# The last batch of a fused graph layer: first picked rows transposed and split inside the gates, last state turned back two products on, second-layer banks in a new order

## The chip, the cores and the metric

One Trainium2 chip, one of its cores. The metric is the device time of one execution in microseconds (us), as the median of several runs. All eight batches of the problem are worked on by this one core, one behind the other.

The engines are named as the profile names them: PE is the matrix engine (PEld its weight loads), DVE the vector engine, ACT the scalar engine, POOL the GpSimd engine, SP the queue that issues the transfers. An order such as `up` or `gelu` is a function of the kernel; its line numbers are those of the kernel before.

## The reference

Two layers with a residual each. The second one is what the change is about: it runs on rows picked by a learned weight.

```
x = x + gnn(layernorm(x), adj, ...)          # 8 x 1024 x 128
x = x + ffn(layernorm(x), ...)

# the end of gnn: a GRU cell
gi = x_in @ w_ih.T + b_ih ;  gh = x @ w_hh.T + b_hh
r = sigmoid(gi_r + gh_r) ;  z = sigmoid(gi_z + gh_z)
n = tanh(gi_n + r * gh_n)
return (1 - z) * n + z * x

# ffn: only the rows with the greatest weights, 511 of the 1024 of a batch
weights = x @ wr + br
idx  = top_k(weights, 512)[:, :511]
sel  = x[idx]
y    = (gelu(sel @ w1 + b1) @ w2 + b2) * weights[idx]
return x with y added at idx
```

## The kernel before

Each engine has its own program, written out by hand in order, and they meet at semaphores (`wait_ge`). An engine does nothing behind an instruction that waits. The graph layer is computed batch by batch (`step`, 8 times) with features on the 128 partitions and nodes along the free axis in two halves of 512. At the end of a batch come the **gates**: `gru` and `gru_rest` multiply, for half 0 and then half 1, the weights of the reset, update and new gate into the banks M0, M1, D0, D1 (half 0) and C0, C1, N0, N1 (half 1). Each product of float32 quality is three matmuls (`three`, L1361 to L1363), since both operands are kept as a coarse part and a rest (`xTH` and `xTL`). ACT applies the tanh of the gates (`gates`: `ga` L815, `tr` L818, `tz` L820), DVE adds up the new gate (`new_gate`, L1039 and L1042), ACT takes its tanh (`candidate`, L825), POOL forms state less candidate (`state_less_candidate`, L520), DVE blends (`blend`, L1048 and L1050), PE turns the new state back to nodes (`state_back`, L1455, eight transposes into two banks) and DVE adds it to x (`state_to_nodes`, L1081). Of the last batch there follow DVE's statistics (`moments2` L937, `mean_and_variance` up to `ve` L951), POOL's power (`inv_std2`, L534), and on DVE the norm (`last_norm`, L1300), the node weights (`node_weights`, L1116 to L1119), the base rows (L1315) and the ranks.

Behind the eight batches come nine **groups** of 512 picked rows (`over_groups`, `ffn_step`): groups 0 to 6 are the picked rows of batches 0 to 6, loaded from DRAM by SP (`load_sel`, L433) into the buffer of the adjacency, groups 7 and 8 are all rows of the last batch, whose unpicked rows are masked at the end. A group is: four transposes into bank D0 (`sel_to_features`, L1593), a coarse copy by ACT (`hi_of_sel`, L880) and the rest by DVE (`lo_of_sel`, L1258), four products up (`up`, three matmuls each, banks in rotation over `up_banks`), gelu on ACT (`gelu`, L887) and four products down (`down`, L1615, a float32 matmul that the trace shows as x2). `up(b, p, j)` waits for `lo_of_sel` of its group, and for the gelu that frees its bank; `down(b, p, j)` waits for the gelu of its tile. The picked rows of a group need the ranks of a batch, which DVE finds with counts over the row of weights (`rank`, L1129, L1135 and L1136; tile t takes three of them). In the last batch DVE has ranks of batch 6 between the steps of the gates: 1 to 3 before `new_gate(7, 0)`, 4 and 5 around `blend(7, 0)`, 6 and 7 in `ffn_step` 0, ahead of `blend(7, 1)`, `lo_of_sel` of group 1 and `state_to_nodes`.

In `ffn_step` 0 the PE does: `sel_to_features(0)`, three `up`, then for j = 0 the fourth `up`, `down`, `sel_to_features(1)` and `state_back(7)`; for j = 1 `down` and the first `up` of group 1; for j = 2 and 3 an `up` of group 1 and a `down` each.

Of the kernel before, what the change touches and what calls it, by code (L numbers as in the profile page):

```python
# [143 lines left out]
def build(nc, x, adj, vectors, weights, conv2_w, const, out):  # L144
    ctx = ExitStack()
    with ctx:
# [161 lines left out]

        up_banks = (C0, C1, D1)
        LU = len(up_banks)  # L310

        def wait(eng, s, b, per, k):
# [351 lines left out]
        def _(act):  # L664
# [144 lines left out]
            def gates(b, h):  # L809
# [10 lines left out]
                nc.scalar.activation(tz[:, h, :], z[:, :], ACT.Tanh, bias=col(V_GB + 1), scale=0.5).then_inc(tz_ok, 1)  # L820

            def candidate(b, h):
                wait(act, q2_ok, b, NH, h + 1)
                wait(act, back_ps, b - 1, NH, NH)
                nc.scalar.activation(gn[:, h, :], ga[:, h, :], ACT.Tanh, bias=col(V_BIH + 2)).then_inc(gn_ok, 1)  # L825
# [13 lines left out]
            def step(b, q, first, last):  # L839
# [31 lines left out]
                gates(b, 0)  # L871
                candidate(b, 0)
                gates(b, 1)

            over_batches(act, step)


            def hi_of_sel(b, p):
                wait(act, t_ps, b, 1, 1)
                nc.scalar.activation(xTH[:, 0, half(p)], D0[:, :], ACT.Copy).then_inc(xsH_ok, 1)  # L880

# [13 lines left out]
            def ffn_step(b, q, first, last):  # L895
                if first:
                    hi_of_sel(0, 0)
                gelu(b, q, 0)
                if first:
                    candidate(B - 1, 1)  # L900
                    hi_of_sel(1, 1)
                gelu(b, q, 1)
                gelu(b, q, 2)
                if not first and not last:
                    hi_of_sel(b + 1, 1 - q)
                if b == 2:
                    row_of_weights(B - 1, 0, M1)
                if not first:
                    update(b - 1, 1 - q)
                gelu(b, q, 3)  # L910
                if b == 2:
                    row_of_weights(B - 1, 1, M1)
# [6 lines left out]
        def _(dve):  # L919
# [108 lines left out]
            def common_added(b, k):  # L1028

                wait(dve, cc_ps, b, 2, k + 1)  # L1030
                wait(dve, g1_ok, b, 1, 1)
                cc = (N0[:, Q:2 * Q], N1[:, 0:Q])[k]
                STT(phases(GS[k]), on_phases(cc), col(V_SC2), phases(G1), ALU.mult, ALU.add).then_inc(gs_ok, 1)  # L1033

            def new_gate(b, h):
# [130 lines left out]
            def step(b, q, first, last):  # L1166
# [79 lines left out]
                blend(b, 0)  # L1246
                if last:
                    rank(b - 1, 0, 5)
                elif not first:
                    rank(b - 1, 1 - q, 4)  # L1250
                    indices(b - 1, 1 - q, 0)

            over_batches(dve, step)


            def lo_of_sel(b, p):
                wait(dve, xsH_ok, b, 1, 1)
                TT(xTL[:, 0, half(p)], D0[:, :], f32(xTH[:, 0, half(p)]), ALU.subtract).then_inc(xsL_ok, 1)  # L1258

# [59 lines left out]
            def ffn_step(b, q, first, last):  # L1319
                if first:  # L1320
                    new_gate(B - 1, 1)
                    lo_of_sel(0, 0)
                    rank(B - 2, 0, 6)
# [32 lines left out]
        def _(pe):  # L1356
# [75 lines left out]
            def conv_odd(b):  # L1432
# [16 lines left out]
                i.then_inc(c2_ps, 1)  # L1449

            def state_back(b, bank_):
                for h in range(NH):
                    wait(pe, o_ok, b, NH, NH)
                    for k in range(TH):
                        i = TR(bank_[h][:, k * P:(k + 1) * P], gn[:, h, k * P:(k + 1) * P], ident)  # L1455
                    i.then_inc(back_ps, 1)
# [81 lines left out]
            def gru_rest(b, h, q, parts, last):  # L1538
# [6 lines left out]
                else:  # L1545
                    wait(pe, nmL_ok, b, NH, NH)
                three(nh[:, :], wh(2), *X, True, True).then_inc(gate_ps, 1)
                three(ni[:, :], wi(2, 0), *XC, True, False)
                wait(pe, nmL_ok, b, NH, h + 1)
# [32 lines left out]

            def sel_to_features(b):
                if b < NXS:
                    pe.wait_ge(sel_in[b], 16)
                else:
                    pe.wait_ge(xn2_ok, B)
                if b == 0:
                    pe.wait_ge(q2_ok, NH * (B - 1) + 1)
                wait(pe, xsL_ok, b - 1, 1, 1)  # L1590
                for c in range(TH):
                    rows = Xs[:, b, c, 0:D] if b < NXS else R[:, 1, (b - NXS) * TH + c, 0:D]
                    i = TR(D0[:, c * P:(c + 1) * P], rows, ident)  # L1593
                i.then_inc(t_ps, 1)

            def up(b, p, j):
                wait(pe, xsL_ok, b, 1, 1)
                k = HT * b + j
                if k < LU:
                    pe.wait_ge((tr_ok, tz_ok, ga_ok)[k], NH * B if k < 2 else NH * (B - 1) + 1)  # L1600
                else:
                    pe.wait_ge(g_ok, k - LU + 1)
# [25 lines left out]
            def ffn_step(b, q, first, last):  # L1628
                if first:
                    sel_to_features(0)  # L1630
                    for k in range(LU):
                        up(0, 0, k)
                for j in range(HT):
# [5 lines left out]
                    if first and j == 0:  # L1639
                        sel_to_features(1)  # L1640
                        pe.wait_ge(tz_ok, NH * (B - 1) + 1)
                        pe.wait_ge(ga_ok, NH * B)
                        state_back(B - 1, (M1, N1))
                    if first and j == 1:
                        up(1, 1, 0)
                    if j == 1 and not first:
# [32 lines left out]
```

## Time and profile before

| | |
|---|---|
| Median of 3 runs | 565.66 us (565.02 to 565.83) |
| The profiled execution's own time | 567.16 us |
| Its span in the trace | 564.2 us |
| PE busy | 546.7 us, 97% of the span |
| DVE busy | 481.7 us, 85% |
| ACT busy | 354.2 us, 63% |
| POOL busy | 275.9 us, 49% |
| Mean granted clock of PE | 0.993 of full speed |

The trace begins with the first instruction and ends with the last; some 3 us of the profiled execution's time lie outside it. A row of the timeline gives start and duration in us, engine, line, operation, written tile <- read tiles, shape and count; in square brackets stands how long the engine had been idle and what released it. Buffer numbers are left out there, so that D is D0 or D1. Instructions of one engine overlap a little: the next one starts some 0.1 us (DVE, ACT) or 0.16 us (PE) before the one ahead of it ends. A row of the windows gives a stretch, its length, the busy time of PE, PEld, DVE, ACT and POOL with their instructions, then the granted clock of PE (1.00 is 2.4 GHz, 0.50 is 1.2 GHz), the DMA share and GB/s.

### The profile page before, as it was taken

Reading aid. Unit: us, or ns where it says so; the run is one execution under the profiler, and the core shown is the slowest. Engines: PE = TensorE matmul, PEld = TensorE weight load, DVE = VectorE, ACT = ScalarE, POOL = GpSimd, SP = SyncE. Lnnn points to the kernel's source line nnn. Section 1 sums busy time; section 2 is a strip of 40 time slices with the busy share of each in tenths; the row PEclk is TensorE's granted clock in tenths of the full one; section 3 lists DMA queues with packets and bytes.
Section 4 is the critical chain, followed back from the end, with each engine's and each line's share of the span. In section 5 each row is a group of like instructions: output and inputs, shape, how many; then the busy total and the mean of one; then the engine's idle time right before and its main releaser. Section 6 shows DMA issues by size and latency. Waiting matters only on the chain.

```text
span 564.2 us, 9042 instructions
## 1 busy us (share of the span) xinstructions
PE 546.7 (97%) x2964; PEld 417.2 (74%) x2964; DVE 481.7 (85%) x1064; ACT 354.2 (63%) x616; POOL 275.9 (49%) x346
## 2 busy tenths in 40 slices
PE   6899999999999999999999999999999999899996
PEld 3786788678966896689767976798678866666563
DVE  6997479689998999899999999899979987978722
ACT  4856475856686577748674858485857573555552
POOL 2740353325368335834484547554535265546552
PEclk9899999999999999999999999999999999999999
DMA  8602700180008300640056002800180006402111
GB/s 290 261 1 76 299 0 2 46 309 20 2 0 281 130 2 1 220 192 1 1 142 268 1 2 59 316 2 1 46 314 15 1 4 192 142 16 80 34 37 60
DMA packets 33339, 54.52 MB, mean 97 GB/s; under 512 B 2098, under 2 KB 23051, under 8 KB 33166
## 3 DMA queue, kind: packets, MB, share of 16 engines
q1 hardware_dynamic: 29710, 48.42, 24.6%
q0 software_dynamic: 3584, 5.54, 2.8%
q8 instruction: 23, 0.38, 0.3%
q14 instruction: 22, 0.18, 0.1%
HBM read 44.21 MB, written 13.43 MB: 102 GB/s over the span
## 4 chain that ended last, share of the span: by engine, by line
PE 84%; DVE 10%; ACT 3%; issue 2%; DMA 0%; POOL 0%; DVEq 0%; ACTq 0%; POOLq 0%
PE N L1510 19%; PE M L1487 10%; PE C L1361 7%; PE C L1362 7%; PE C L1363 7%; PE N L1615 6%; PE D L1481 5%; PE N L1361 3%; PE N L1362 3%; PE N L1363 3%; ACT hab L671 2%; DVE tr L1011 2%; PE D L1361 2%; PE M L1362 2%; PE M L1361 2%
## 5 line engine op out<-in xcount | busy, mean ns | idle before, releaser
L777 ACT ACTIVATE tr<-D 128x512 f32<-128x512 f32 x128 | 76.2, 596 | 76.8 <-PE D L1481 70.0
L1487 PEld LDWEIGHTS M<-cst,adjb 128*128 128x128 f32 x512 | 63.7, 141 | 36.5 <-issue 19.8
L1481 PE MATMUL D<-V,U 128*128 128x512 f32 x128 | 89.3, 697 | 0.0
L1487 PE MATMUL M<-cst,adjb 128*128 128x128 f32 x512 | 76.9, 273 | 1.3 <-DVE ga L1105 0.9
L575 POOL DMA_INDIRECT sel<-R,ridx x56 | 61.2, 1092 | 16.0 <-issue 13.8
L1510 PE MATMUL N<-tz,msgF 128*128 128x512 f32 x128 | 64.2, 593 | 0.0
L1510 PE MATMUL N<-ga,msgF 128*128 128x512 f32 x128 | 64.2, 593 | 0.0
L1361 PE MATMUL C<-zR,wc 128*128 128x256 f32 x208 | 61.0, 293 | 0.0
L1362 PE MATMUL C<-zR,wc 128*128 128x256 f32 x208 | 58.9, 283 | 0.0
L1363 PE MATMUL C<-zR,wc 128*128 128x256 f32 x208 | 58.8, 283 | 0.0
L1135 DVE TENSOR_SCALAR_CACHE_REDUCE junk<-W,R 128x1024 bf16<-128x1024 f32 (+3 forms) x64 | 51.6, 807 | 3.9 <-ACT W L739 2.1
L1105 DVE TENSOR_TENSOR ga<-tr,M 128x512 f32<-128x512 f32 x64 | 43.5, 680 | 10.7 <-ACT tr L777 10.0
L1105 DVE TENSOR_TENSOR tz<-tr,M 128x512 f32<-128x512 f32 x64 | 43.6, 683 | 7.3 <-ACT tr L777 3.3
L621 POOL TENSOR_TENSOR wk<-tz,xT 128x512 f32<-128x512 f32 x8 | 12.5, 1566 | 70.8 <-DVE tz L1033 70.8
L520 POOL TENSOR_TENSOR ga<-xT,gn 128x512 f32<-128x512 f32 x16 | 22.8, 1424 | 44.9 <-ACT gn L825 44.1
L1129 DVE TENSOR_SCALAR_CACHE_REDUCE junk<-W,R 128x128 bf16<-128x128 f32 (+6 forms) x56 | 41.3, 738 | 0.0
L1481 PEld LDWEIGHTS D<-V,U 128*128 128x128 f32 x128 | 24.3, 190 | 22.9 <-ACT tr L777 17.4
L602 POOL TENSOR_TENSOR junk<-hab 128x521 f32<-128x521 f32 x16 | 20.1, 1258 | 41.5 <-ACT hab L671 41.5
L1362 PEld LDWEIGHTS C<-zR,wc 128*128 128x128 f32 x208 | 39.8, 191 | 0.0
L1361 PEld LDWEIGHTS C<-zR,wc 128*128 128x128 f32 x208 | 39.6, 190 | 0.2 <-issue 0.2
L1363 PEld LDWEIGHTS C<-zR,wc 128*128 128x128 f32 x208 | 39.7, 191 | 0.0
L586 POOL DMA_INDIRECT out<-xn,adjb x28 | 28.4, 1014 | 20.8 <-DVE xn L1290 14.4
(237 smaller groups left out, 1537.1 us busy)
## 6 DMA issues: line engine op xcount, KB each, us to landing
adjb<-in_adj SPq DMA_DIRECT2D x8, 4096.0 KB, 14.9
adjb<-sel SPq DMA_DIRECT2D x7, 516.0 KB, 5.8
xall<-in_x SPq DMA_DIRECT2D x7, 512.0 KB
out<-R SPq DMA_DIRECT2D x7, 512.0 KB
R<-in_conv_w SPq DMA_DIRECT2D x1, 1088.0 KB, 6.9
sel<-R,ridx POOLq DMA_INDIRECT x56
xall<-in_weights SPq DMA_DIRECT2D x1, 832.0 KB, 9.4
xall<-in_x SPq DMA_DIRECT2D x2, 256.0 KB, 2.7
```

Of the source, the lines that this page charges most:

```text
L575: nc.gpsimd.indirect_dma_start(sel[b], bass.IndirectOffsetOnAxis(ap=ridx[:, q, t:t + 1], axis=0), R[:, q, t, :], None, bounds_check=KEEP - ...
L777: nc.scalar.activation(E[:, u % NE, :], Db[u % NH][:, :], ACT.Exp, scale=-1.0).then_inc(exp_ok, 1)
L1105: TT(A[u % NA], E[:, u % NE, :], Mb[u % NH][:, :], ALU.mult).then_inc(A_ok, 1)
L1129: TS(junk[:, t % 2, 0:t * P], W[:, 0:t * P], R[:, q, t, R_W:R_W + 1], None, ALU.is_ge, ALU.add, accum_out=acc[:, 0, t:t + 1])
L1135: TS(junk[:, k, t * P:N], W[:, t * P:], w, None, ALU.is_gt, ALU.add, accum_out=acc[:, 1, t:t + 1])
L1361: MM(out_, wgt(0), hi, start=start, stop=False)
L1362: MM(out_, wgt(0), lo, start=False, stop=False)
L1363: return MM(out_, wgt(1), hi, start=False, stop=stop)
L1481: MM(Db[h][:, :], U[:, t * P:(t + 1) * P], V[:, half(h)], start=True, stop=True).then_inc(d_ps, 1)
L1487: i = TR(Mb[h][:, k * P:(k + 1) * P], adjb[:, h * TH + k, t * P:(t + 1) * P], ident)
L1510: MM(Nb[h][:, :], msgF[:, t, :], A[v % NA], start=t == 0, stop=t == T - 1).then_inc(nm_ps, 1)
L1615: i = MM(Nb[p][:, :], wf2[:, j, :], g[p][j], start=j == 0, stop=j == HT - 1)
```

## The change

It touches only the end of the last batch and the first group.

1. **First picked rows.** `sel_to_features(0)` moves on PE from behind the gates into those of the second half, behind the state's product of the new gate (`nh`, bank N1), and writes bank M0 in place of D0 (`sel_bank`). `hi_of_sel(0, 0)` moves on ACT from behind the last gates to between `candidate(7, 0)` and `gates(7, 1)`. `lo_of_sel(0, 0)` moves on DVE from behind `new_gate(7, 1)` to behind `blend(7, 0)`, ahead of `rank` 5.
2. **Banks.** `up_banks` is (D1, C0, C1) in place of (C0, C1, D1), so that the first product up doesn't wait for the gates of the second half.
3. **State back.** `state_back(7)` moves on PE from behind `sel_to_features(1)` to behind `down(0, 2)`.

No instruction is added or taken away.

```
-        up_banks = (C0, C1, D1)
+        up_banks = (D1, C0, C1)
...
+        def sel_bank(b):
+            return M0 if b == 0 else D0
...
                 gates(b, 0)
                 candidate(b, 0)
+                if last:
+                    hi_of_sel(0, 0)
                 gates(b, 1)
...
                 blend(b, 0)
                 if last:
+                    lo_of_sel(0, 0)
                     rank(b - 1, 0, 5)
...
+            def sel_to_features(b):
+                if b < NXS:
+                    pe.wait_ge(sel_in[b], 16)
+                else:
+                    pe.wait_ge(xn2_ok, B)
+                if b == 0:
+                    pe.wait_ge(tr_ok, NH * (B - 1) + 1)
+                if b == 1:
+                    pe.wait_ge(q2_ok, NH * (B - 1) + 1)
...
                 three(nh[:, :], wh(2), *X, True, True).then_inc(gate_ps, 1)
+                if last and h == 1:
+                    sel_to_features(0)
                 three(ni[:, :], wi(2, 0), *XC, True, False)
...
-                    pe.wait_ge((tr_ok, tz_ok, ga_ok)[k], NH * B if k < 2 else NH * (B - 1) + 1)
+                    pe.wait_ge((ga_ok, tr_ok, tz_ok)[k], NH * B if k > 0 else NH * (B - 1) + 1)
...
                 if first:
-                    sel_to_features(0)
                     for k in range(LU):
                         up(0, 0, k)
...
                     if first and j == 0:
                         sel_to_features(1)
+                    if first and j == 1:
+                        up(1, 1, 0)
+                    if first and j == 2:
                         pe.wait_ge(tz_ok, NH * (B - 1) + 1)
                         pe.wait_ge(ga_ok, NH * B)
                         state_back(B - 1, (M1, N1))
-                    if first and j == 1:
-                        up(1, 1, 0)
```

PE in the gates of the second half, before and after (L1363 and L1367 end the new gate's product of the state, N0 takes its part of the convolved features, C0 the reset gate's part of the messages):

```order
L1363 MATMUL N1<-xTH,wall 128x512
L1361 MATMUL N0<-zR,wall 128x512
L1362 MATMUL N0<-zR,wall 128x512
L1363 MATMUL N0<-zR,wall 128x512
L1361 MATMUL C0<-V,wall 128x512
```

```order
L1367 MATMUL N1<-xTH,wall 128x512
L1467 MATMUL M0<-cst,adjb 128x128 x4
L1365 MATMUL N0<-zR,wall 128x512
L1366 MATMUL N0<-zR,wall 128x512
L1367 MATMUL N0<-zR,wall 128x512
L1365 MATMUL C0<-V,wall 128x512
```

The four transposes of the first picked rows now stand ahead of twelve matmuls of the gates.

PE in the first group, from `down(0, 0)` on, before and after (L1615 and L1623 are products down, L1593 and L1467 the picked rows of group 1, L1455 and L1474 the state):

```order
L1615 MATMUL N0<-xall,msgF 128x512
L1593 MATMUL D0<-cst,adjb 128x128 x4
L1455 MATMUL M1<-cst,gn 128x128 x4
L1455 MATMUL N1<-cst,gn 128x128 x4
L1615 MATMUL N0<-xall,msgF 128x512
L1361 MATMUL C1<-xTH,wall 128x512
L1362 MATMUL C1<-xTL,wall 128x512
L1363 MATMUL C1<-xTH,wall 128x512
L1361 MATMUL D1<-xTH,wall 128x512
```

```order
L1623 MATMUL N0<-xall,msgF 128x512
L1467 MATMUL D0<-cst,adjb 128x128 x4
L1623 MATMUL N0<-xall,msgF 128x512
L1365 MATMUL C0<-xTH,wall 128x512
L1366 MATMUL C0<-xTL,wall 128x512
L1367 MATMUL C0<-xTH,wall 128x512
L1365 MATMUL C1<-xTH,wall 128x512
L1366 MATMUL C1<-xTL,wall 128x512
L1367 MATMUL C1<-xTH,wall 128x512
L1623 MATMUL N0<-xall,msgF 128x512
L1474 MATMUL M1<-cst,gn 128x128 x4
L1474 MATMUL N1<-cst,gn 128x128 x4
```

Behind the picked rows of group 1 there is now nothing between the transposes and `down(0, 1)`; the state stands two products up and one product down later.

ACT from the candidate of the first half on, before and after (L815 and L819 are `ga`, L880 and L828 the coarse copy of picked rows):

```order
L825 ACTIVATE gn<-ga,vec 128x512
L815 ACTIVATE ga<-N1,vec 128x512
L818 ACTIVATE tr<-C0,vec 128x512
L820 ACTIVATE tz<-C1,vec 128x512
L880 ACTIVATE xTH<-D0 128x512
L887 ACT_TABLE_LOAD
L887 ACTIVATE xall<-C0,vec 128x512
```

```order
L833 ACTIVATE gn<-ga,vec 128x512
L828 ACTIVATE xTH<-M0 128x512
L819 ACTIVATE ga<-N1,vec 128x512
L822 ACTIVATE tr<-C0,vec 128x512
L824 ACTIVATE tz<-C1,vec 128x512
L893 ACT_TABLE_LOAD
L893 ACTIVATE xall<-D1,vec 128x512
```

The copy of the first picked rows now stands ahead of the three gates of the second half, and the load of the gelu table right behind them.

## Rows read from the trace of the kernel before

**Rows 1.** The page, the chain that ended last by engine.
```profile
PE 84%; DVE 10%; ACT 3%; issue 2%; DMA 0%; POOL 0%; DVEq 0%; ACTq 0%; POOLq 0%
```

**Rows 2.** Timeline of PE, last gates and first group: start, us, engine, instruction.
```profile
484.21 0.39 PE L1361 MATMUL N<-zR,wall 128*128 128x512 f32 x1
...
489.74 0.50 PE L1361 MATMUL C<-xTH,wall 128*128 128x512 f32 x1 [2.15 <-DVE xTL L1258]
...
495.08 0.60 PE L1593 MATMUL D<-cst,adjb 128*128 128x128 f32 x4
...
496.95 1.12 PE L1615 MATMUL N<-xall,msgF 128*128 128x512 f32 x2 [0.39 <-ACT xall L887]
...
498.14 0.40 PE L1362 MATMUL C<-xTL,wall 128*128 128x512 f32 x1
```

**Rows 3.** Windows: length, busy of PE, PEld, DVE, ACT, POOL, then granted clock.
```profile
8.00:11.31 3.31, 1.28 (x8) 0.87 (x9) 3.08 (x11) 1.97 (x4) 1.63 (x5) 1.00 1.03 337
17.00:19.00 2.00, 0.00 (x0) 0.00 (x0) 2.00 (x2) 0.57 (x1) 2.00 (x2) 1.00 1.02 408
20.50:23.30 2.80, 2.80 (x14) 2.62 (x14) 2.80 (x3) 2.75 (x5) 2.72 (x3) 0.50 0.90 358
491.30:494.40 3.10, 3.10 (x8) 2.27 (x7) 3.03 (x9) 0.74 (x2) 1.28 (x1) 0.50 0.00 1
```

**Rows 4.** Timeline of ACT, end of the gates.
```profile
486.49 0.69 ACT L820 ACTIVATE tz<-C,vec 128x512 f32<-128x512 f32 x1
487.63 0.60 ACT L880 ACTIVATE xTH<-D 128x512 fp32r<-128x512 f32 x1 [0.45 <-issue]
488.24 1.28 ACT L887 ACT_TABLE_LOAD   x1
```

**Rows 5.** SP's loads of picked rows: forms, first and last start, time to landing.
```profile
L433 SPq DMA_DIRECT2D adjb<-sel x7: 359/427/523, 471.2 to 509.3; - x7
...
DMA to landing us min/median/max: 4.2/5.8/7.2
```

**Rows 6.** Timeline of DVE, from the blend of the first half on.
```profile
485.46 0.69 DVE L1050 SCALAR_TENSOR_TENSOR gn<-ga,gn 128x512 f32<-128x512 f32 x1
...
489.00 0.68 DVE L1258 TENSOR_TENSOR xTL<-D,xTH 128x512 fp32r<-128x512 f32 x1
...
492.53 1.02 DVE L1136 SCALAR_TENSOR_TENSOR junk<-W,R,cst 128x128 bf16<-128x128 f32 x1
...
494.60 0.69 DVE L1050 SCALAR_TENSOR_TENSOR gn<-ga,gn 128x512 f32<-128x512 f32 x1
496.35 0.69 DVE L1258 TENSOR_TENSOR xTL<-D,xTH 128x512 fp32r<-128x512 f32 x1 [1.06 <-ACT xTH L880]
496.96 0.68 DVE L1081 TENSOR_TENSOR xall<-xall,M 128x512 f32<-128x512 f32 x1
```

**Rows 7.** Line L1136 from 475 to 495 us: least, median and greatest ns.
```profile
L1136 DVE SCALAR_TENSOR_TENSOR junk<-W,R,cst x7: 344/347/1033, 477.2 to 492.5; 128x128 bf16<-128x128 f32 x7
```

**Rows 8.** Timeline of POOL: state less candidate, and the power of the statistics.
```profile
492.13 1.28 POOL L520 TENSOR_TENSOR ga<-xT,gn 128x512 f32<-128x512 f32 x1 [1.64 <-ACT gn L825]
...
500.91 1.67 POOL L534 TENSOR_TENSOR rstd<-ve,vec 128x8 f32<-128x8 f32 x1 [7.51 <-DVE ve L951]
```

**Rows 9.** Timeline of DVE, statistics, norm and rows of the last batch.
```profile
500.67 0.17 DVE L951 TENSOR_TENSOR ve<-vsum,mdif 128x8 f32<-128x8 f32 x1
503.00 0.69 DVE L1258 TENSOR_TENSOR xTL<-D,xTH 128x512 fp32r<-128x512 f32 x1 [2.16 <-ACT xTH L880]
503.60 2.13 DVE L1300 TENSOR_SCALAR R<-xall,mean,rstd 128x128 f32<-128x128 f32 x8
...
510.73 0.68 DVE L1258 TENSOR_TENSOR xTL<-D,xTH 128x512 fp32r<-128x512 f32 x1
```

**Rows 10.** Timeline of PE, the first products up of groups 3 and 4.
```profile
511.74 0.48 PE L1361 MATMUL C<-xTH,wall 128*128 128x512 f32 x1
...
519.34 0.50 PE L1361 MATMUL C<-xTH,wall 128*128 128x512 f32 x1 [0.27 <-issue]
```

More of the change, by code:

```diff
@@ L820, in gates, with hi_of_sel @@
                 nc.scalar.activation(tz[:, h, :], z[:, :], ACT.Tanh, bias=col(V_GB + 1), scale=0.5).then_inc(tz_ok, 1)
+            def hi_of_sel(b, p):
+                wait(act, t_ps, b, 1, 1)
+                nc.scalar.activation(xTH[:, 0, half(p)], sel_bank(b)[:, :], ACT.Copy).then_inc(xsH_ok, 1)
             def candidate(b, h):
@@ L872, in step @@
                 candidate(b, 0)
+                if last:
+                    hi_of_sel(0, 0)
                 gates(b, 1)
             over_batches(act, step)
-            def hi_of_sel(b, p):
-                wait(act, t_ps, b, 1, 1)
-                nc.scalar.activation(xTH[:, 0, half(p)], D0[:, :], ACT.Copy).then_inc(xsH_ok, 1)
             def gelu(b, p, j):
@@ L895, in ffn_step @@
             def ffn_step(b, q, first, last):
-                if first:
-                    hi_of_sel(0, 0)
                 gelu(b, q, 0)
@@ L1033, in common_added, with lo_of_sel @@
                 STT(phases(GS[k]), on_phases(cc), col(V_SC2), phases(G1), ALU.mult, ALU.add).then_inc(gs_ok, 1)
+            def lo_of_sel(b, p):
+                wait(dve, xsH_ok, b, 1, 1)
+                TT(xTL[:, 0, half(p)], sel_bank(b)[:, :], f32(xTH[:, 0, half(p)]), ALU.subtract).then_inc(xsL_ok, 1)
             def new_gate(b, h):
@@ L1253, in _ @@
             over_batches(dve, step)
-            def lo_of_sel(b, p):
-                wait(dve, xsH_ok, b, 1, 1)
-                TT(xTL[:, 0, half(p)], D0[:, :], f32(xTH[:, 0, half(p)]), ALU.subtract).then_inc(xsL_ok, 1)
             def kept_weights():
@@ L1321, in ffn_step @@
                     new_gate(B - 1, 1)
-                    lo_of_sel(0, 0)
                     rank(B - 2, 0, 6)
@@ L1449, in conv_odd @@
                 i.then_inc(c2_ps, 1)
+            def sel_to_features(b):
[7 more added lines that the diff above has]
+                    pe.wait_ge(q2_ok, NH * (B - 1) + 1)
+                wait(pe, xsL_ok, b - 1, 1, 1)
+                for c in range(TH):
+                    rows = Xs[:, b, c, 0:D] if b < NXS else R[:, 1, (b - NXS) * TH + c, 0:D]
+                    i = TR(sel_bank(b)[:, c * P:(c + 1) * P], rows, ident)
+                i.then_inc(t_ps, 1)
             def state_back(b, bank_):
@@ L1580, in _ @@
             over_batches(pe, step)
[L1583 to L1594, printed above, removed]
             def up(b, p, j):
```

## The prediction

> **What bounds the kernel now.** I read the page's chain first: 84% of it is PE [rows 1]. So the end moves with PE as long as nothing else is late. Then the timeline of PE where the change works, from the last gates to the first products of the second layer. It stands still there twice: 2.15 us for `lo_of_sel(0, 0)`, and 0.39 us for the gelu in front of `down(0, 1)` [rows 2]. Behind the first pause the clock falls to 0.50 (1.2 GHz): all of 491.30 to 494.40 runs at half speed, eight matmuls in 3.10 us [rows 3]. That is another 1.5 us, so the place holds some 4 us. The question is how much of it PE can have back, and for that the timelines of DVE, ACT and POOL have to be laid beside it: DVE works nearly without a break up to the blend of the second half, whose last instruction starts at 494.60 [rows 6].
>
> **The first picked rows, on PE.** The four transposes now start at 484.21, where the matmuls on N0 stood [rows 2]. They take 0.60 us [rows 2], of which 0.16 overlaps with what follows, so they push the gates by 0.44. They are added there and gone from behind the gates. Their wait is for the rows: SP issued the load at 471.2 and the slowest of the seven landed after 7.2 us, so by 478.4 [rows 5]; cover 5.8 us. If the load were late, all gates of the second half would queue behind it. The bank M0 is free once the first half's `tr` is read, long before. `up(0, 0, 0)` then follows the gates: the 2.15 us pause began at 487.59, the transposes ahead of it 0.60 earlier at 486.99 [rows 2], plus 0.44 is **487.43**.
>
> **On ACT.** `hi_of_sel` starts as the transposes end, 484.81, and takes 0.60 [rows 4]: 485.45. Queued behind it are the three gates of the second half. The first of them slips by a microsecond, but the last is bound by PE: 486.49 plus 0.44 [rows 4] is 486.93, ended at 487.62. Behind it stands the table load, 1.28 us [rows 4], ended at 488.90, and then the first gelu, 0.69 like `tz` (same shape and form): 489.59. So the gelu is bound by the table and no longer by PE.
>
> **On DVE.** `lo_of_sel(0, 0)` follows the blend: 485.46 plus 0.60 is 486.06, ended 486.74, in time for 487.43. Rank 5 and `new_gate(7, 1)` come 0.60 later and end when `lo_of_sel` ended before, at 489.60 [rows 6]. From there DVE has the same work in the same order as before: ranks 6 and 7, indices, blend. So **nothing that waits for the second half's blend comes earlier than DVE lets it**. `lo_of_sel(1, 1)` waited 1.06 us for ACT [rows 6]; now it can start right behind the blend, 494.60 plus 0.60 is 495.20, ended 495.89.
>
> **The new banks.** D1 is free since the first half, C0 since the second half's `tr` and C1 since its `tz` at 487.62, which `up(0, 0, 2)` needs at 488.83. Cost nothing, cover 1.2 us; if it fails, PE waits for ACT by what is missing.
>
> **The first group on PE.** A product up is three matmuls 0.23 apart (0.39 less the overlap of 0.16), 0.70. Three of them end at 489.53. The fourth waits for the first gelu and runs from 489.65 to 490.40. `down(0, 0)` takes 0.86 (the 1.12 of [rows 2] less 0.16 of overlap and the 0.1 of a start from rest): 491.26. Then the picked rows of group 1. From these transposes to `down(0, 1)` it was 495.08 to 496.95, 1.87 us at full clock [rows 2], a chain over ACT (copy, gelu) that nothing shortens; `state_back` used to lie under it and now doesn't. So `down(0, 1)` starts at 493.13 after a **pause of 1.27**. It ends at 494.25, and `up(1, 1, 0)` waits for `lo_of_sel(1, 1)`, to 495.95: a **pause of 1.70**. Its second matmul is at 496.29, and was at 498.14 [rows 2]: a lead of 1.85 us. Of the 4 us no more can be had, since DVE ends it. And `state_back`, eight transposes or 0.88, is still to be done. What is left to PE is 1.85 - 0.88 = 0.97.
>
> **What is late next.** The state. It follows `up(1, 1, 0)` (0.80 from rest), `up(1, 1, 1)` (0.70) and `down(0, 2)` (0.86): it starts at 498.31, its first half is done at 498.91, and DVE adds it from 498.95 on, where it was 496.96 [rows 6]: **1.99 later**. Behind it hang in a row the statistics up to `ve` (500.67, now 502.66, ended 502.83), POOL's power, 1.67 us [rows 8], now 502.90 to 504.57, and the norm of the last batch, 503.60 [rows 9], now 504.60. DVE had 2.16 us of slack ahead of `lo_of_sel(2)` [rows 9], which takes the 1.99; that order even starts at 502.75 in place of 503.00, so PE still leads by 0.25 at `up(2, 0, 0)`. But the norm is **1.00 late**, for POOL stands between. From 503.60 to 510.73 DVE had no idle figure in any row [rows 9], so `lo_of_sel(3)` goes from 510.73 to 511.73, ended 512.41, and the first product up of group 3, at 511.74 before [rows 10], starts at 512.47: 0.73 late. The old order rested 0.27 ahead of 519.34 [rows 10], which takes some of it. I count the rest, 0.46, to the end, where PE is the chain.
>
> The sum against the profiled execution (567.16, span 564.20): 567.16 + 0.46 = 567.6. The median of the runs is 1.50 below that execution; I carry the difference over: 565.66 + 0.46 = **566.1**. Its unknowns: each hand-over between engines (0.04 to 0.06 here) and the later slack, in which 0.3 either way, and the clock, which is a rival.
>
> **A place where POOL and DVE meet.** Seven runs of L1136 take 344 to 1033 ns with a median of 347 [rows 7]; the 1.02 us one at 492.53 lies under POOL's subtraction of 492.13 to 493.41 [rows 8]. That subtraction follows `candidate(7, 1)`, which now comes right behind the first gelu, at about 489.7, ended 490.4. POOL subtracts from 490.5 to 491.8, over the L1136 of rank 6 instead of rank 7: the same 0.68 us, paid once. So I count nothing. The Trainium skill, "GPSIMD Engine Reference", section "Key points", says that the two engines contend for the memory interfaces where the vector instruction has two inputs there, which L1136 has. By that rule a start of POOL that meets neither would give the 0.68 back; the trace agrees in that the counts of one input beside it keep their time.
>
> **Rivals.**
> (1) *The clock falls behind the new pauses*: the slower side. In the trace it fell behind 2.15 us of rest, and behind a rest that holds all of 17.00 to 19.00, with 0.50 from 20.50 to 23.30; it did not fall in 8.00 to 11.31, where PE was busy for 1.28 of 3.31 us between several shorter rests [rows 3]. The new pauses are 1.27 and 1.70 with 1.12 of work between: each is shorter than those that made it fall, both together (2.97 of 4.09 us) are more. If it falls at about 496, the 2.36 us of work up to the state run at half speed, and state, statistics, norm and everything behind them come 1.1 to 1.7 later, 1.45 in the middle: 566.1 + 1.45 = 567.5. It decides from the point where the fall lies ahead of 498.3; behind it PE has 0.6 of slack ahead of `up(2, 0, 0)`. The Trainium skill, "TensorE: Matmul & The Clock Gate", section "Why this matters for your kernels", warns of one long gap between bursts of matmuls; by that alone two short ones would do nothing, and the time would stay at 566.1. The fall behind 2.15 us in this trace makes me less sure.
> (2) *PE keeps its lead*: the norm isn't late enough to matter, since ranks or base rows have slack that I don't see. Then the 0.97 stay: 564.7. For it speaks the chain, 84% PE; against it POOL's 1.67 us and a DVE without idle time for 7 us. It decides where the state comes less than 1 us late on DVE.
> (3) *POOL meets neither L1136*: all from 495.20 on comes 0.68 earlier, 565.4.
> (4) *The change doesn't do what it says*, as the picked rows are late in the gates. The load has 5.8 us of cover; I give it next to nothing.
>
> **How the numbers follow.** The forecast 0.42, (1) 0.37, (2) 0.12, (3) 0.06, others 0.03. The likeliest gives 566.1, its own range is 565.7 to 566.6. Range to hold 8 in 10: from (2), 564.7, to the upper part of (1), 567.8. A measurement of this kernel tells about 0.2% from no change, here 564.5 and 566.8. Faster than that are a good third of (2), a little of (3) and the others, 0.09; slower are nearly all of (1), 0.37; the same 0.54.
>
> **What the profile of the changed kernel would show.** PE: the transposes of the first rows among the last gates, no pause of 2 us behind them, then one of 1.3 ahead of `down(0, 1)` named ACT gelu, and one of 1.7 ahead of `up(1, 1, 0)` named DVE `lo_of_sel`. ACT: the table load straight behind `tz`, the first gelu straight behind that. DVE: no idle time ahead of `lo_of_sel(1, 1)`, idle time ahead of `state_to_nodes`, and about 1.1 us of it ahead of the norm, behind POOL's power. The windows from 491 to 500: clock 1.00 throughout for the forecast, a stretch of 0.50 for (1). It would be wrong if the state's transposes reached DVE before 498, or if `up(1, 1, 0)` started far from 2 us ahead of its old place.

## Result and profile after

| | before | changed |
|---|---|---|
| Median | 565.80 us (565.02 to 567.20, 20 runs) | 568.03 us (566.16 to 569.73, 20 runs) |
| Ratio | | 1.0034, 95% interval 1.0026 to 1.0043 |
| The profiled execution | 567.16 us | 569.6 us |
| Its span | 564.2 us | 567.0 us |

The changed kernel is **slower**, by 0.34% (1.9 us by the ratio, 2.2 by the medians). The forecast called likeliest, 566.1, is not what came. In the profiled execution it is the first rival, the clock that falls behind the new pauses. In the experiments below, one of the eleven executions of e6 (1156 us) and one of the kernel before beside it (690.6 us) count in no ratio.

The median of 568.03 hides that the 20 runs lie in two bunches of ten, with nothing between 567.78 and 568.28:

| changed kernel | runs | times | median | mean granted clock of each run |
|---|---|---|---|---|
| lower bunch | 10 | 566.16 to 567.78 us | 566.84 us | 0.995 or 0.996 |
| upper bunch | 10 | 568.28 to 569.73 us | 568.44 us | 0.991 to 0.994 |

The profiled execution (0.991) is of the upper bunch. The traces of e1, e7 and e11, which have no fall from 490 to 504, have 0.995 or 0.996, like the lower bunch; each of them has one fall near the start of the kernel (between 11 and 25 us), and so does the profiled execution. So the late fall came in about half of the runs, and 568.03 is the middle of the gap. This is read from the clocks; no execution of the lower bunch was profiled.

PE after, from the last gates on (timeline: start, us, engine, instruction, idle time before it and what ended it). It answers to [rows 2].

```profile
484.37 0.60 PE L1467 MATMUL M<-cst,adjb 128*128 128x128 f32 x4
...
487.62 0.40 PE L1365 MATMUL D<-xTH,wall 128*128 128x512 f32 x1
...
491.60 0.60 PE L1467 MATMUL D<-cst,adjb 128*128 128x128 f32 x4
493.46 1.12 PE L1623 MATMUL N<-xall,msgF 128*128 128x512 f32 x2 [1.27 <-ACT xall L893]
496.08 0.80 PE L1365 MATMUL C<-xTH,wall 128*128 128x512 f32 x1 [1.49 <-DVE xTL L1041]
...
498.80 1.91 PE L1623 MATMUL N<-xall,msgF 128*128 128x512 f32 x2
500.50 1.06 PE L1474 MATMUL M<-cst,gn 128*128 128x128 f32 x4
...
506.25 0.50 PE L1365 MATMUL C<-xTH,wall 128*128 128x512 f32 x1 [0.44 <-DVE xTL L1041]
...
512.51 0.62 PE L1482 MATMUL M<-cst,R 128*128 128x128 f32 x4 [0.45 <-DVE R L1127]
```

The 2.15 us pause is gone, and in its place stand the two that the prediction named: 1.27 us ahead of `down(0, 1)`, 1.49 us ahead of `up(1, 1, 0)`. Behind them a product down takes 1.91 us instead of some 1.1: the clock is low. The windows of the same execution say so (length, busy of PE, PEld, DVE, ACT, POOL, granted clock):

```profile
491.60:493.40 1.80, 0.59 (x5) 0.36 (x3) 1.80 (x7) 1.17 (x3) 0.32 (x1) 1.00 0.00 0
493.40:494.60 1.20, 1.12 (x2) 0.30 (x2) 1.13 (x7) 1.17 (x3) 0.00 (x0) 1.00 0.00 0
494.60:496.00 1.40, 0.00 (x0) 0.00 (x0) 1.37 (x3) 0.00 (x0) 0.00 (x0) 0.69 0.00 0
496.00:502.00 6.00, 5.92 (x16) 4.21 (x17) 0.42 (x2) 1.38 (x2) 0.00 (x0) 0.50 0.01 3
502.00:506.00 4.00, 3.81 (x16) 2.19 (x15) 3.86 (x18) 2.40 (x4) 0.33 (x1) 1.00 0.00 0
```

The clock falls inside the second pause and stays at 1.2 GHz for all of 496 to 502. In the kernel before it was low over 491.30 to 494.40 [rows 3]. DVE and POOL, behind the state (answers to [rows 6], [rows 8] and [rows 9]):

```profile
495.34 0.68 DVE L1041 TENSOR_TENSOR xTL<-D,xTH 128x512 fp32r<-128x512 f32 x1
501.60 0.69 DVE L1089 TENSOR_TENSOR xall<-xall,M 128x512 f32<-128x512 f32 x1 [5.58 <-PE M L1474]
...
507.37 2.14 DVE L1305 TENSOR_SCALAR R<-xall,mean,rstd 128x128 f32<-128x128 f32 x8 [1.18 <-POOL rstd L538]
...
514.51 0.68 DVE L1041 TENSOR_TENSOR xTL<-D,xTH 128x512 fp32r<-128x512 f32 x1
```

```profile
490.65 1.27 POOL L524 TENSOR_TENSOR ga<-xT,gn 128x512 f32<-128x512 f32 x1 [0.39 <-ACT gn L833]
505.67 1.67 POOL L538 TENSOR_TENSOR rstd<-ve,vec 128x8 f32<-128x8 f32 x1 [13.75 <-DVE ve L955]
```

The state is added at 501.60, where it was 496.96, the norm starts at 507.37 where it was 503.60. DVE rests for 5.58 us in front of the state.

Executions differ by tenths in where the last batch begins, so the traces below are laid together from one point that no kernel here moves: the start of DVE's first rest of the messages (L1118, L1110 before) in the last gates. State, norm and end are the starts of `state_to_nodes`, of `last_norm` and of DVE's last masked rows (L1283, L1278 before), in us from that point. In the changed kernel these are

```profile
474.58 0.69 DVE L1118 TENSOR_TENSOR U<-N,V 128x512 fp32r<-128x512 f32 x1 [0.85 <-ACT V L811]
...
562.96 1.12 DVE L1283 SCALAR_TENSOR_TENSOR R<-M,kept,R 128x128 f32<-128x128 f32 x4 [2.09 <-PE M L1633]
```

so the end is at 88.38 us. The other rows of the table are read in the same way.

| one profiled execution each | state on DVE | norm | end | clock at 490 to 504 |
|---|---|---|---|---|
| before | 22.51 | 29.15 | 85.80 | falls |
| changed | 27.02 | 32.79 | 88.38 | falls |
| changed, again (e12) | 26.10 | 31.77 | 88.31 | falls |
| changed, both pauses filled (e1) | 24.48 | 30.15 | 85.76 | 1.00 |
| second pause filled (e7) | 24.48 | 30.15 | 86.56 | 1.00 |
| first pause filled (e11) | 24.48 | 30.15 | 86.69 | 1.00 |
| before, its pause filled (e4) | 21.67 | 28.44 | 84.61 | 1.00 |
| before, late state alone (e5) | 24.77 | 30.44 | 86.84 | 1.00 |
| changed, old place of the state (e6) | 21.65 | 28.42 | 84.92 | 1.00 |
| changed, state behind down(0, 1) (e2) | 21.92 | 29.16 | 85.37 | falls |
| the same, filled (e3) | 21.66 | 27.57 | 83.72 | 1.00 |
| changed, rank 7 later (e8) | 22.65 | 29.08 | 85.57 | 1.00 |
| both cures (e9) | 20.48 | 26.91 | 83.54 | 1.00 |
| both cures, filled (e10) | 20.40 | 26.84 | 83.49 | 1.00 |

### The profile page after: what moved, and what is told of

Same layout as the page of the kernel before. It is cut to its first block, busy times and chain, and to the rows that moved or that the text cites. A ratio compares the mean times of both kernels' runs of the same rounds, so it can differ in the third digit from the quotient of the medians.

```text
span 567.0 us, 9042 instructions
## 1 busy us (share of the span) xinstructions
PE 548.6 (97%) x2964; PEld 417.8 (74%) x2964; DVE 482.0 (85%) x1064; ACT 354.5 (63%) x616; POOL 275.5 (49%) x346
## 4 chain that ended last, share of the span: by engine, by line
PE 79%; DVE 12%; issue 4%; ACT 3%; POOL 1%; DMA 1%; DVEq 0%; ACTq 0%; POOLq 0%
PE N L1529 19%; PE M L1506 10%; PE C L1365 6%; PE C L1366 6%; PE C L1367 6%; PE D L1500 5%; PE N L1623 4%; PE N L1365 3%; PE N L1366 3%; PE N L1367 3%; ACT hab L675 2%; DVE tr L1015 2%; PE M L1366 2%; PE M L1365 2%; PE M L1367 2%
## 5 line engine op out<-in xcount | busy, mean ns | idle before, releaser
L1367 PE MATMUL C<-zR,wc 128*128 128x256 f32 x208 | 58.9, 283 | 0.0
L1367 PEld LDWEIGHTS C<-zR,wc 128*128 128x128 f32 x208 | 39.7, 191 | 0.0
```

Source lines behind the costliest of these rows:

```text
L1367: return MM(out_, wgt(1), hi, start=False, stop=stop)
```

## Experiments

Theory C: the clock takes most of the loss, and the late state the rest. Rival S: the late state takes all of it, and the clock only shifts waits. "Unread" matmuls are extra work whose result goes into a bank that nobody reads; they keep PE busy in a pause and carry no data. Each time below stands against the kernel before on the same chip. There were three chips: one for e1 to e4, one for e5 to e8, one for e9 to e12; of the runs of the result and the two traces that belong to them, the chip isn't known.

### e1: both pauses filled

```
+            def fill(n):
+                pe.wait_ge(tz_ok, NH * (B - 1) + 1)
+                for _ in range(n):
+                    MM(M1[:, :], weight(W_C1)(0), wall[:, 0, W_F1:W_F1 + HALF], start=True, stop=True)
...
+                    if first and j == 1:
+                        fill(5)
                     down(b, q, j)
...
                     if first and j == 1:
+                        fill(6)
                         up(1, 1, 0)
```

> The changed kernel with eleven more matmuls on PE, whose result nobody reads: five (128x512, written into the idle bank M1) in the pause ahead of down(0, 1) and six in the pause ahead of up(1, 1, 0). They carry no data and lengthen nothing if they fit (0.23 us each, 1.2 us into 1.27 and 1.4 us into 1.49). Theory C (of the 2.2 us that the change costs, the clock that falls behind the two pauses takes about 1.7, and the late state the rest): the granted clock stays 1.00 from 490 to 500 and the time is 0.3 to 0.7 above the kernel before, about 566.3. Rival S (the whole loss is the late state and what hangs behind it, the fall only shifts waits): the clock stays up too, but the time stays within 0.4 of the changed kernel, about 567.8.

Measured 566.41 us (11 runs) against 565.80, ratio 1.0013 (1.0004 to 1.0022). The timeline of PE:

```profile
492.33 1.40 PE L1639 MATMUL M<-wall 128*128 128x512 f32 x5
493.84 1.13 PE L1623 MATMUL N<-xall,msgF 128*128 128x512 f32 x2
494.40 1.95 PE L1639 MATMUL M<-wall 128*128 128x512 f32 x6
496.53 0.50 PE L1365 MATMUL C<-xTH,wall 128*128 128x512 f32 x1 [0.18 <-DVE xTL L1041]
...
498.88 0.60 PE L1474 MATMUL M<-cst,gn 128*128 128x128 f32 x4
```

Eleven matmuls more, and the kernel is 1.6 us faster than the changed one (2.2 above the kernel before there, 0.6 here; by the ratios, 1.0034 and 1.0013, it is 1.2). The window from 490 to 504 has clock 1.00. `up(1, 1, 0)` starts 21.49 us from the common point, and in the changed kernel 21.50, so nothing else was changed but the clock. S, which expected about 567.8, falls. C holds for the net loss; what the late state costs by itself is in e3.

### e7, e11: one pause filled

The same edit with only the six, or only the five.

> The changed kernel with six unread matmuls in its second pause alone, ahead of up(1, 1, 0); the first, of 1.27 us, stays. Theory C, if the two pauses act together: what is left is one pause of 1.3 us and one of 0.1, the clock holds in nearly all runs, 566.4 as with both filled. If the first pause alone makes the clock fall: a stretch of 0.50 and 567 to 568.

> The changed kernel with five unread matmuls in its first pause alone, ahead of down(0, 1); the second, of 1.49 us ahead of up(1, 1, 0), stays. If the two pauses act together, the clock holds in nearly all runs and the time is within 0.3 of the kernel in which the second alone is filled, about 1.0 above the kernel before. If the second is the one that counts, the clock falls and it stays at 2 above.

With the second filled 567.18 us (567.03 to 567.74, 11 runs) against 566.14, ratio 1.0020 (1.0011 to 1.0029): a narrow spread, clock 1.00 in the trace. With the first filled 567.63 (567.02 to 569.86, 10 runs) against 566.21, ratio 1.0032 (1.0020 to 1.0045): eight runs within 567.0 to 568.1, two at 569.5 and 569.9; the profiled one, 567.16, has clock 1.00. So the longer pause alone may make it fall in a few runs (none of those was profiled), the shorter one shows no sign of it in eleven, and the two together do it in about half. Both times were expected too low against the kernel before beside them, by 0.4 in the medians (1.0 above it for 0.6, 1.4 for 1.0): see the second path in the next section.

### e12: the changed kernel again

> The changed kernel itself once more, beside the three others on one chip. By theory C the profile shows either a stretch of 0.50 behind the second pause or none, and the time of the profiled execution goes with it: with a fall the state reaches DVE at 500.5 or later, without one at about 499, and the difference is 1.1 to 2.5 us.

568.89 us (567.26 to 569.85, 6 runs) against 566.21, ratio 1.0041 (1.0025 to 1.0057); four runs are at 568.89 or more, two at 567.66 or less. In the profiled one (569.1) the clock fell again, later and for a shorter time, so that the state came 1.6 after the 24.48 of e1, not 2.5:

```profile
496.00:498.00 2.00, 1.53 (x4) 1.21 (x5) 0.42 (x1) 0.17 (x1) 0.00 (x0) 0.72 0.04 8
498.00:500.00 2.00, 2.00 (x5) 1.23 (x4) 0.00 (x0) 1.20 (x2) 0.00 (x0) 0.50 0.00 0
500.00:502.00 2.00, 2.00 (x12) 1.44 (x11) 0.92 (x2) 0.00 (x0) 0.00 (x0) 0.92 0.00 0
```

A profile of the changed kernel without a fall was not caught; e1, e7 and e11 stand in for it.

### e4: the kernel before with its pause filled

```
                 if first:
                     sel_to_features(0)
+                    fill(8)
                     for k in range(LU):
```

> The kernel before with eight unread matmuls (1.9 us) in its pause of 2.15 us ahead of up(0, 0, 0). Theory C: no fall of the clock at 491; the PE work up to the state is 1.5 us earlier, but the state then waits for the blend (495.3), so about 0.8 us are left: 565.0, and the runs spread less than those of the kernel before. Rival S: the fall was hidden under DVE anyway, no change, 565.8.

565.63 us (11 runs) against 565.80, ratio 0.9994 (0.9985 to 1.0002): not told apart. The profile has clock 1.00 and ends 1.19 earlier from the common point (84.61, 85.80). Of that, 0.73 is the fall, and 0.46 is a wait for stores that the trace of the kernel before has besides (the second path of the next section). The highest run is 565.91, the highest of before 566.69. The fall in the kernel before costs something when it comes, but it seems not to come in every run, so its median shows little of it: of the 35 runs of the kernel before on that chip, the 17 with a mean clock of 0.997 or 0.998 have a median of 565.35, the 18 with 0.992 to 0.995 one of 566.06. The expected 565.0 is the level of the five fastest of the eleven runs.

### e5: the late state alone

The kernel before with `state_back(B - 1, (M1, N1))` and its waits moved from j = 0 to j = 2 behind `down`.

> The third part of the change alone: the kernel before with state_back(7) behind down(0, 2), first picked rows and banks as they were. Theory C with the late state: the state reaches DVE at about 500.7 in place of 497.0, the norm of the last batch is 2.8 late, and with 0.7 us of slack the end is some 2.0 later, 567.8, though the clock falls once at 491 as in the kernel before. If instead the order of the picked rows is what costs, this is no slower than 566.2.

568.07 us (567.25 to 569.46, 5 runs) against 566.14, ratio 1.0036 (1.0022 to 1.0049). This part alone makes the kernel as slow as the whole change. Its profile has no fall in this place, and its end is 86.84 against the 84.61 of e4, 2.2 us later. That isn't all PE: its transposes for the rows of group 2 start 1.4 later than in e4 (47.26, 45.83), and 0.8 is a wait for stores that e4, on another chip, doesn't have.

```profile
489.81 0.50 PE L1361 MATMUL C<-xTH,wall 128*128 128x512 f32 x1 [2.15 <-DVE xTL L1258]
495.43 1.13 PE L1615 MATMUL N<-xall,msgF 128*128 128x512 f32 x2 [1.26 <-ACT xall L887]
498.64 0.60 PE L1455 MATMUL M<-cst,gn 128*128 128x128 f32 x4
```

```profile
490.00:492.00 2.00, 2.00 (x9) 1.60 (x9) 2.00 (x7) 1.19 (x2) 0.56 (x1) 1.00 0.12 41
492.00:494.00 2.00, 2.00 (x10) 1.25 (x8) 1.93 (x9) 0.11 (x1) 1.27 (x1) 1.00 0.00 0
```

The pause of 2.15 us is the one of [rows 2], same place and length, and here the clock stays at 1.00 behind it.

### e6: the other two parts alone

The changed kernel with `state_back` and its waits back behind `sel_to_features(1)`.

> The first two parts alone: the changed kernel with state_back(7) back behind sel_to_features(1). PE then stands still in one piece for the blend, from about 491.9 to 495.4, so the clock falls in nearly every run, but the state comes at 496.1 to 496.5, as early as in the kernel before. Up(1, 1, 0) keeps 0.7 us of its lead and loses up to 1.7 to the fall: 566.0 to 566.8, so 1.2 to 2 us less than the changed kernel. If the first picked rows in the gates were the harmful part, it would be no better than 567.5.

567.47 us (11 runs) against 566.14, ratio 1.0026 (1.0017 to 1.0036): worse than expected. One run has 565.34, nine have 566.9 to 568.4. The profiled one is the 565.34, with a pause of 3.40 us and no fall:

```profile
495.60 0.63 PE L1474 MATMUL M<-cst,gn 128*128 128x128 f32 x4 [3.40 <-DVE gn L1058]
...
494.00:496.00 2.00, 0.41 (x4) 0.44 (x5) 1.97 (x4) 0.57 (x1) 0.00 (x0) 1.00 0.00 0
496.00:498.00 2.00, 2.00 (x12) 1.44 (x10) 1.75 (x6) 0.00 (x0) 0.00 (x0) 1.00 0.03 8
```

So where the clock holds, the first two parts with the state at its old place cost nothing and gain nothing: PE's transposes for the rows of group 2 start at 45.81, in e4 at 45.83, since PE waits for the blend either way; and 565.34 is level with the fastest run of the kernel before on that chip, 565.38. The other nine are 1.5 to 3.1 us slower. That these are the runs with a fall is argued from e1; none of them was profiled. The expected price of a fall, 1.0 to 1.7 less the lead, was too low here too.

### e2, e3: the state between down(0, 1) and up(1, 1, 0)

```
                     if first and j == 1:
+                        pe.wait_ge(tz_ok, NH * (B - 1) + 1)
+                        pe.wait_ge(ga_ok, NH * B)
+                        state_back(B - 1, (M1, N1))
                         up(1, 1, 0)
-                    if first and j == 2:
-                        pe.wait_ge(tz_ok, NH * (B - 1) + 1)
-                        pe.wait_ge(ga_ok, NH * B)
-                        state_back(B - 1, (M1, N1))
```

> The changed kernel with state_back(7) between down(0, 1) and up(1, 1, 0), ahead of both products up and the product down behind which the change put it. It waits there for the blend, to about 495.4, so the two pauses stay nearly as long, and the clock can fall as before. Theory C: the state reaches DVE at about 496.1 at full clock, 5.5 us before the changed kernel, so that a fall no longer delays statistics and norm but only PE, by at most 1.7 us, of which the lead of 1.5 us pays most: 565.0 to 566.2. Rival S predicts the same sign from the state alone and more of it, whatever the clock does: 564.5 to 565.0 in all runs.

> As the one before (state_back(7) between down(0, 1) and up(1, 1, 0)), with five unread matmuls in the pause ahead of down(0, 1) and four in the one ahead of state_back. Theory C: the clock stays at 1.00; DVE has the state 0.9 us earlier than the kernel before, and PE a lead of 1.5: 0.9 to 1.2 us below the kernel before, 564.6 to 564.9, and the spread of the runs is under 0.6 us. Rival S: no different from the kernel without the unread matmuls.

Unfilled 564.87 us (12 runs) against 565.80, ratio 0.9989 (0.9979 to 0.9999). The runs lie in two bunches, six from 564.12 to 564.47 and six from 565.28 to 566.55; the profiled one has 565.86 and shows the fall (0.50 over 496 to 498). The median is a little below C's range and within that of S, 564.5 to 565.0, but S expected it of all runs. Filled 564.43 (564.16 to 564.95, 11 runs), ratio 0.9980 (0.9971 to 0.9989), a gain of 1.4 by the medians and 1.1 by the ratio for the expected 0.9 to 1.2; the spread of 0.8 is wider than the expected 0.6, but **the upper bunch is gone**. That the lower bunch of e2 is the one without a fall follows from this and isn't in a trace of its own.

Three filled kernels on this one chip, all with clock 1.00 and without a wait for stores, take the change apart:

| clock 1.00, same chip | end | median |
|---|---|---|
| kernel before, filled (e4) | 84.61 | 565.63 us |
| changed, state behind down(0, 1), filled (e3) | 83.72 | 564.43 us |
| changed, filled (e1) | 85.76 | 566.41 us |

The first two parts gain 0.9 in the traces (1.2 in the medians) once the state isn't put behind them. The late place of the state costs **2.0 us** (2.0 in the medians), the greatest single price, and the lead pays about half of it. What is left is 1.2 in the traces and 0.8 in the medians; the rest of the loss is the clock.

### e8: rank 7 behind the norm's statistics

```
                     rank(B - 2, 0, 6)
-                    rank(B - 2, 0, 7)
-                    indices(B - 2, 0, 1)
                     blend(B - 1, 1)
...
                 if b == 1:
+                    rank(B - 2, 0, 7)
+                    indices(B - 2, 0, 1)
                     last_norm()
```

> The changed kernel with rank 7 of batch 6 and its indices (2.3 us of DVE) moved from ahead of blend(7, 1) to behind lo_of_sel(2), where DVE waited for POOL. The step of the prediction that is tried is that DVE alone ends the lead of PE: then up(1, 1, 0) starts about 1.7 us earlier, at 494.4, its pause is gone, the clock holds, and the state comes at 497.2. The norm then stands behind rank 7, 0.4 late: 565.5 to 566.1. If the pause ahead of up(1, 1, 0) has another cause, it stays, and the time with it, at 568.

566.30 us (566.00 to 567.08, 11 runs) against 566.14, ratio 1.0001 (0.9992 to 1.0010). `lo_of_sel(1, 1)` starts at 493.66 in place of 495.34, PE has no pause ahead of `up(1, 1, 0)` and the clock is 1.00.

```profile
493.66 0.68 DVE L1041 TENSOR_TENSOR xTL<-D,xTH 128x512 fp32r<-128x512 f32 x1
```

So it was DVE that ended the lead. The whole loss goes with one order moved on DVE, while PE keeps the change's own order. That isn't a second proof of e1, since this edit takes away both causes at once: the pause, and 1.8 us of the state's lateness (22.65 for 24.48).

### e9, e10: both cures

As e2, and rank 7 with its indices behind `mean_and_variance`; e10 with the five unread matmuls ahead of `down(0, 1)` too.

```
                     blend(B - 1, 1)
                     lo_of_sel(1, 1)
                     state_to_nodes(B - 1, (M1, N1))
                     moments2(B - 1)
                     mean_and_variance(1, stats2, T * B)
+                    rank(B - 2, 0, 7)
+                    indices(B - 2, 0, 1)
```

> Both cures of the late state in the changed kernel: rank 7 of batch 6 and its indices behind mean_and_variance, and state_back(7) between down(0, 1) and up(1, 1, 0). The blend is then done at 493.5, down(0, 1) ends at 494.3, so there is no second pause, and DVE has the state at about 495.0 in place of 497.0 in the kernel before. Rank 7 stands where DVE waited for POOL. Norm, node weights and all behind them come 1.6 to 1.9 earlier: 1.4 to 2.0 us below the kernel before. If the norm is bound elsewhere, by PE above all, it is no more than 1.2.

> As the one before (rank 7 behind mean_and_variance, state_back(7) behind down(0, 1)), with five unread matmuls in the one pause of 1.27 us that is left. If one pause of that length doesn't make the clock fall, the two have the same median within 0.2 us and the same spread. If it does in part of the runs, this one is up to 1 us below the other's median.

e9: **564.12 us** (563.79 to 565.42, 9 runs) against 566.21, ratio 0.9968 (0.9958 to 0.9978), 2.1 us below the kernel before and 4.8 below the changed one on this chip (e12). e10: 564.25 (6 runs), 0.9969 (0.9958 to 0.9981). The medians don't differ, so one pause of 1.26 us does no harm in most runs, as in e7; whether the two slowest of e9, 565.20 and 565.42, had a fall isn't known. DVE in e9:

```profile
493.32 0.68 DVE L1041 TENSOR_TENSOR xTL<-D,xTH 128x512 fp32r<-128x512 f32 x1
495.05 0.69 DVE L1089 TENSOR_TENSOR xall<-xall,M 128x512 f32<-128x512 f32 x1 [1.05 <-PE M L1474]
...
501.48 2.13 DVE L1305 TENSOR_SCALAR R<-xall,mean,rstd 128x128 f32<-128x128 f32 x8
```

The state comes 1.9 earlier than in [rows 6], the norm 2.1 earlier than in [rows 9], and nothing in it waits for POOL any more, since rank 7 fills that time.

## Why the prediction was right or wrong

The sum with the late state came out almost to a tenth, and the first rival, which was to make the kernel slower by a fall of the clock, is what the upper ten runs show. The range to 567.8 holds the ratio (1.0034 on the 565.66 from which the sum started is 567.6), but the median of 568.03 lies 0.2 above it, and it stands in a gap in which no run was. With one run more in the lower bunch it would have been 567.8, with one more in the upper one 568.3; that the number lies so near the edge of the range is luck either way.

**The steps up to 496.** Nearly all came to a tenth. The transposes start at 484.37 (predicted 484.21, but the batch began 0.13 later); `up(0, 0, 0)` at 487.62 (487.43); the pause ahead of `down(0, 1)` is 1.27 (1.27); `lo_of_sel(1, 1)` at 495.34 without idle time (495.20). The pause ahead of `up(1, 1, 0)` is 1.49 (1.70), as the four products up had been summed 0.2 too short. The load of the picked rows and the new banks cost nothing: no row of PE names them in front of these orders. POOL's subtraction now lies over the L1144 of rank 6, which takes 1.01 us at 491.06, and that of rank 7 takes 0.34 at 493.34: paid once, as said.

**The late state.** Right in mechanism and nearly in size where the clock holds. Predicted 1.99 later than before; in e1, e7 and e11 it is 24.48 against 22.51, so 1.97. The norm was to be 1.00 late, with POOL between: 30.15 against 29.15, so 1.00, and the idle figure is the 1.18 named POOL. PE then does not wait at the first product of group 3 but a little before, at the row of weights (0.45), by the same chain. The orders on PE that the sum followed are 0.74 and 0.43 late in e1 (37.29 to 38.03 and 44.89 to 45.32 from the common point), where it had 0.73 and 0.46. e1 has 0.61 in the medians. But the sum set a changed kernel without a fall against an execution of before that had one. Against a kernel before whose clock holds as well, the changed one ends 1.15 later (e1 and e4), and the place of the state alone costs 2.0 (e1 and e3).

**A second path that the sum lacks.** e7 and e11 end 0.8 to 0.9 later than e1 with the state and norm at the same place. In e11 DVE's rows of group 2 start at 523.24, though PE's transposes for them (521.63, 0.60) ended at 522.23. That order also waits for the stores of group 0, which POOL issues behind `inv_std2`, and that waits for the state. POOL's fourth store and DVE's rows, first of e1, then of e11:

```profile
516.13 0.97 POOL L590 DMA_INDIRECT out<-xn,adjb  x1 [0.30 <-DVE xn L1295]
522.66 1.13 DVE L1295 SCALAR_TENSOR_TENSOR xn<-M,adjb 128x128 f32<-128x128 f32 x4 [0.74 <-PE M L1633]
```

```profile
515.74 0.97 POOL L590 DMA_INDIRECT out<-xn,adjb  x1 [0.30 <-issue]
523.24 1.13 DVE L1295 SCALAR_TENSOR_TENSOR xn<-M,adjb 128x128 f32<-128x128 f32 x4 [1.72 <-PE M L1633]
```

POOL issues the store equally late in both, 41.09 and 41.08 from the common point, and 1.0 later than in the kernel before (40.07). In e1 that costs nothing: DVE goes on 6.53 us behind it, as soon as PE is done. In e11 it goes on only after 7.50. In the nine traces in which DVE waits here beyond PE, before and e5 to e12, this time is 7.34 to 7.59 whatever PE does. In the other five, the changed kernel and e1 to e4, it isn't what DVE waits for. The trace names PE as what released it; that it is the landing of a store is an inference from these times. So the late state has a second way to the end, over POOL's queue, which binds in some executions and not in others; all four traces of one chip are without it and all eight of the two others have it. I had written that DVE's chain is what follows the state and had not followed POOL's queue to its stores.

**The clock: where the likeliest case failed.** What failed is the choice between two cases, not a cost up to the state: I gave 0.42 to "the clock holds" and 0.37 to its fall, and took one of them for all runs. It falls in about half of them. What spoke for holding was that each new pause is shorter than any that was followed by a fall; in e7 and e11, with one pause left, the profiled clock holds, and both profiled falls of the changed kernel follow pauses of 1.3 and 1.5 us with 1.1 us of work between them. The Trainium skill, "TensorE: Matmul & The Clock Gate", section "Why this matters for your kernels", warns of one long gap between bursts of matmuls; by that alone nothing would have happened here. These two traces don't agree with it.

**Its price** was predicted at 1.1 to 1.7, with 1.45 in the middle. The two bunches are 1.6 apart, within that. Single executions differ: in e12 the state came 1.62 later than in e1, and in the profiled execution 2.54, outside. There the clock was low from the second pause to 502, so that all of the 2.36 us of work up to the state ran at half speed; a price of 1.7 at most presumes a fall that ends before the state, about as long as the one of [rows 3]. The end of that execution is 2.6 later than in e1 (88.38, 85.76), all of it by the clock, for it has no wait for stores. e12 ends 2.55 later, 1.6 by the clock and 0.9 by that wait. The upper bunch, 568.4, is 0.9 above the rival's 567.5. Most of this is the level without a fall: the lower bunch is 1.0 above the median of the kernel before, where the sum had 0.46. The store wait could be the cause, but with no trace of the lower bunch that stays open.

**Why a fall is dearer than before.** In the kernel before the slow stretch lay ahead of the blend, for which the state waited anyway: the state is at 22.51 with the fall and at 21.67 without (e4), so the fall costs it 0.8 us. The change moves the pauses behind DVE's last step, so that the slow stretch lies on PE's way to the state, and adds three orders to that way (two products up and one down).

## What to carry to other kernels

When work is moved off a pause of the bounding engine, look what still ends the lead on the others: here DVE's ranks did, and moving one of them won back the whole loss (e8). An order that starts a long chain on other engines (here the last state: statistics, norm, weights, ranks, stores) should not be put behind work that can wait, even where the engine that issues it loses nothing. And the pauses that are left decide about the clock: here two short ones close together cost more in the runs in which the clock fell than the one long one they replaced. Where they can't be closed, filling them is a cheap test of what the clock takes. Look at all runs before the median: one that lies between two bunches describes no run at all. And compare the ends of two traces only after looking for waits that come with the chip and not with the kernel.

## What the runs showed of the hardware

The same pause gives a fall in one execution and none in another: 2.15 us in the kernel before is followed by 0.50, in e5 by 1.00, with PE's orders around it alike; and one of 3.40 us (e6) was followed by 1.00. So a profile of one execution doesn't tell whether a kernel's clock falls, only that it can. All runs together with the filled kernel do: 564.1 to 564.5 and 565.3 to 566.6 in e2, of which only the lower bunch is left in e3. Bunches alone are no proof: e4, whose trace has clock 1.00 here, has runs at 565.0 to 565.2 and at 565.6 to 565.9.

A fall can also last longer than the one before it: in the kernel before all of 491.30 to 494.40 is at 0.50, and 490.00 to 491.00 and what follows 495.00 at 1.00; in the changed one all of 496 to 502 is low, with PE busy for 5.92 of those 6.00 us.

The time from POOL's issue of a store to DVE's going on behind it was 7.34 to 7.59 us in nine traces, and no more than 6.53 and 6.55 in e1 and the changed kernel.
